# A message-passing layer on one Trainium2 core: scatters and gathers in turn, a shorter start

## The reference, cut to what matters

```
rhat = edge_vec / (norm(edge_vec) + 1e-12);  Y1 = sqrt(3) * rhat
emb  = 8 Gaussians of the clipped length, times sqrt(8), zero where length > 1
w    = mlp(emb)                       # 8 -> 64 -> 64 -> 128, silu between
xs, xv = x[:, :32] @ W_up0, x[:, 32:] as (32, 3) by W_up1   # scaled by 32 ** -0.5
m0 = w0 * xs[src];   m1 = w1 * xs[src] * Y1
m2 = w2 * xv[src];   m3 = w3 * sum_c(xv[src] * Y1) / sqrt(3)
msg = segment_sum([m0, m3 | m1, m2], dst)
out = layernorm(x + (msg_s @ W_out0 | msg_v by W_out1) / (8 * 16))
```

## Time and profile before

| what | us |
|---|---|
| median of 3 runs (1263.23 to 1265.73) | 1265.41 |
| the profiled execution | 1268.42 |
| its span, first to last instruction | 1266.7 |
| POOL busy | 995.5 (79%) |
| PE busy | 968.7 (76%) |
| DVE busy | 698.5 (55%) |
| ACT busy | 540.2 (43%) |

### The profile page before, as it was taken

How to read it: one execution, slowest core, us unless ns; L and a number is a source line. 1 busy time by engine, 2 the same in 40 slices (tenths; PEclk the granted TensorE clock), 3 DMA queues, 4 the chain that set the end, 5 groups by cost and what they waited for, 6 DMA issues and landing times.

```text
span 1266.7 us, 31319 instructions
## 1 busy us (share of the span) xinstructions
PE 968.7 (76%) x6210; PEld 893.6 (71%) x6210; DVE 698.5 (55%) x2916; ACT 540.2 (43%) x1416; POOL 995.5 (79%) x792
## 2 busy tenths in 40 slices
PE   1888888787778887788777777888777868888880
PEld 1787777777777776677677676777676767778770
DVE  6764344466465565556555656646546556555532
ACT  4433223244435434525535534534443543553532
POOL 5378887878888888878888888888888888788885
PEclk9988788888877878878888978779878897777785
DMA  6466674434544444543453454444444454453444
GB/s 204 142 183 181 172 196 78 71 72 97 124 71 98 98 98 71 123 99 70 100 123 73 95 124 70 98 99 82 105 105 74 96 122 72 87 134 43 69 68 89
DMA packets 84975, 132.19 MB, mean 104 GB/s; under 512 B 17308, under 2 KB 69935, under 8 KB 84133
## 3 DMA queue, kind: packets, MB, share of 16 engines
q0 software_dynamic: 68304, 50.25, 29.9%
q1 hardware_dynamic: 14506, 78.09, 17.1%
q10 hardware_dynamic: 1963, 1.71, 0.5%
HBM read 78.35 MB, written 77.24 MB: 123 GB/s over the span
## 4 chain that ended last, share of the span: by engine, by line
POOL 42%; issue 26%; DMA 16%; SPq 10%; POOLq 5%; DVE 0%; ACT 0%
POOL acc L603 28%; DMA acc<-msg,index 14%; POOL sender L573 14%; SPq L380 6%; POOLq L579 3%; SPq L376 2%; SPq L404 2%; DMA acc<-in_x_dram 1%; POOLq L601 1%; POOLq L584 1%; POOLq L602 0%; SPq L426 0%; DMA total<-acc 0%; POOLq L88 0%; SPq L412 0%
## 5 line engine op out<-in xcount | busy, mean ns | idle before, releaser
L603 POOL DMA_INDIRECT acc<-msg,index x391 | 623.5, 1595 | 131.1 <-issue 106.9
L573 POOL DMA_INDIRECT sender<-in_x_dram,index x375 | 368.3, 982 | 128.3 <-issue 102.9
L730 PEld LDWEIGHTS ps_sum<-same,mid 128*128 128x128 f32 x1568 | 255.1, 239 | 10.0 <-DVE mid L1164 0.8
L730 PE MATMUL ps_sum<-same,mid 128*128 128x128 f32 x1568 | 260.2, 321 | 0.7 <-DVE mid L1164 0.7
L1149 DVE TENSOR_TENSOR wts<-ps_wts,bias 128x512 f32<-128x512 f32 x98 | 67.8, 692 | 283.5 <-PE ps_wts L717 283.5
L742 PE MATMUL ps_msg<-outw,sumT 128*128 128x64 f32 x1568 | 220.4, 302 | 0.0
L742 PEld LDWEIGHTS ps_msg<-outw,sumT 128*128 128x128 f32 x1568 | 216.1, 221 | 0.0
L1142 DVE TENSOR_TENSOR proj<-ps_up,vec_all 128x384 f32<-128x384 f32 x98 | 54.4, 555 | 223.5 <-PE ps_up L710 187.9
L827 ACT COPY sumT<-ps_sum 128x512 f32<-128x512 f32 x196 | 115.0, 587 | 146.4 <-PE ps_sum L730 143.7
L689 PE MATMUL ps_sT<-ident,sender 128*128 128x128 f32 x376 | 86.8, 307 | 115.1 <-DMA sender<-in_x_dram,index 114.3
L837 ACT COPY msg<-ps_msg 128x128 f32<-128x128 f32 x98 | 26.1, 266 | 336.1 <-DMA acc<-msg,index 243.1
(11 more groups left out here) (144 smaller groups left out, 1084.6 us busy)
## 6 DMA issues: line engine op xcount, KB each, us to landing
acc<-in_x_dram SPq DMA_DIRECT2D x40, 625.0 KB, 4.8
total<-acc SPq DMA_DIRECT2D x30, 832.0 KB, 4.8
out_dram<-normed SPq DMA_DIRECT2D x29, 832.0 KB
by_row<-in_x_dram SPq DMA_DIRECT2D x1408, 0.5 KB
by_row<-in_x_dram ACTq DMA_DIRECT2D x640, 0.5 KB
acc<-msg,index POOLq DMA_INDIRECT x391, 3.4
sender<-in_x_dram,index POOLq DMA_INDIRECT x375, 6.0
out_dram<-normed ACTq DMA_DIRECT2D x1, 832.0 KB
```

The lines of the kernel that those rows point to most:

```text
L573: pool.indirect_dma_start(sender[:, u % SRING, i, :], None, x, bass.IndirectOffsetOnAxis(ap=index[:, u, 0, i:i + 1], axis=0)).then_inc(fet ...
L603: pool.indirect_dma_start(acc, bass.IndirectOffsetOnAxis(ap=index[:, v, 1, i:i + 1], axis=0), msg[:, v % RING, i, :], None, compute_op=ALU.add
L730: mm = pe.matmul(ps_sum[r][:, i, h, :], mid[:, b, 2 * r + i, P * h:P * (h + 1)], same[:, b, 2 * r + i, :], start=True, stop=True)
```

## The change

1. POOL gathers only the first `EARLY` = 4 units ahead of the first scatter. From then on each scatter of unit v is followed by the gather of the same tile of unit v + 5 (in unit 0, by those of units 4 and 5). The next unit's order is loaded before this unit's scatters.
2. `single_rows` has a twin, `rows_at`, that takes byte offsets. The two lists of row numbers that SP and ACT read in the loop are multiplied by 512 once, on DVE (`scale_ids`). The first two units of SP keep `single_rows`.
3. Basis and directions are made for the first 8 units (`NARROW`) at first, for the other 90 between units 2 and 4. The scatter orders follow unit 0 on DVE (their comparisons are inside it); the output weights are scaled after unit 0's second silu; the message of unit 0 has an order of its own on PE and ACT (`first_message`).
4. SP issues the weights before the zero rows and the first two copies of x, and waits for the turning of unit 1 before the next copies; ACT issues eight of the weight loads. The id lists are loaded after the second pair of copies.

```diff
+EARLY = 4
+NARROW = 8
+ROW_BYTES = D * 4
+        x_bytes = x.rearrange("n d -> (n d)").bitcast(U8)
+        def rows_at(engine, kind, u, i, starts, a, n):
+            _, starts = nc.values_load_multi_w_load_instructions(
+                starts[:, a:a + n], engines=(kind,), min_val=0, max_val=(N - 1) * ROW_BYTES, ...)
+            for p in range(n):
+                engine.dma_start(by_row[a + p:a + p + 1, row_slot(u, i), :].bitcast(U8),
+                                 x_bytes[bass.ds(starts[p], ROW_BYTES)].rearrange("(a d) -> a d", a=1)
                                  ).then_inc(row_in[row_slot(u, i)], 16)
...
 # SP
-            sp.wait_ge(zeroed, 1)
-            sp.dma_start(acc[N:N + SPARE, :]..., zeros[:, :, :]).then_inc(spare_rows, 16)
-            for k in range(PIECES_FIRST):
-                copy(k // 2, k % 2, waits=k >= 2)
             sp.wait_ge(consts, 1)
 # up_raw and mlp0_raw (8 DMAs) now count on loaded_up; then bias2 and out_raw (5) on loaded
-            for s in range(2):
-                (mlp1, mlp2, bias0, bias1)
+            sp.wait_ge(zeroed, 1)
+            sp.dma_start(acc[N:N + SPARE, :]..., zeros[:, :, :]).then_inc(spare_rows, 16)
+            for k in range(PIECES_FIRST):
+                copy(k // 2, k % 2, waits=k >= 2)
             sp.wait_ge(src_in, 16)
+            sp.wait_ge(senderT_ps, 2)
...
-                if h == 2 + P // SP_ROWS:
+                if h == 1:
                     load_ids()
...
 # POOL
-            for u in range(AHEAD):
+            for u in range(EARLY):
...
-            orders = [order_of(v) for v in range(ROW)]
-            for v in range(0, UNITS, ROW):
-                for k in range(min(ROW, UNITS - v)):
-                    begin_scatters(v + k, orders[k])
-                    for i in range(G):
-                        scatter(v + k, i, orders[k] % 2)
-                orders = [order_of(w) for w in range(v + ROW, min(v + 2 * ROW, UNITS))]
-                for u in range(v + AHEAD, min(v + AHEAD + ROW, UNITS)):
+            order = order_of(0)
+            for v in range(UNITS):
+                following = order_of(v + 1) if v + 1 < UNITS else None
+                begin_scatters(v, order)
+                ahead = range(v + AHEAD if v else EARLY, min(v + AHEAD + 1, UNITS))
+                for u in ahead:
                     if u >= SRING:
                         pool.wait_ge(senderT_ps, u - SRING + 1)
-                    for i in range(G):
+                for i in range(G):
+                    scatter(v, i, order % 2)
+                    for u in ahead:
                         gather(u, i)
+                order = following
...
 # PE
-            pe.wait_ge(weights, 6)
-            pe.wait_ge(prepared, 2)
-            pe.wait_ge(loaded, 16 * WEIGHT_DMAS)
+            pe.wait_ge(prepared, 1)
+            def first_message(u, k):
+                hidden0(u, k)
+                sums(u - 1, k - 1, 0)
+                sums(u - 1, k - 1, 1)
+                pe.wait_ge(weights, 6)
+                project_out(u - 1, k - 1)
+                project_up(u, k)
+                hidden1(u, k)
+                radial(u, k)
+                turn(u + 1, k + 1)
...
 # ACT
+            act.wait_ge(consts, 1)
+            for h in range(2):
+                (mlp1, mlp2, bias0, bias1: 8 DMAs, ahead of the planes)
...
+            squares(first, range(NB)).then_inc(act_pre, 1)
+            act.activation(basis_all[:, first, :], basis_all[:, first, :], ACT.Exp, scale=-0.5)
...
+                if k == 0:
+                    scale_out()
...
+                if u == 2:
+                    act.wait_ge(dve_pre, LATER_CLIP)
+                    squares(later, range(NB // 2))
+                if u == 3:
+                    squares(later, range(NB // 2, NB)).then_inc(act_pre, 1)
+                if u == 4:
+                    act.activation(basis_all[:, later, :], ..., ACT.Exp, scale=-0.5)
...
 # DVE
+            def scale_ids():
+                dve.wait_ge(ids_in, 16 * len(ID_LISTS))
+                for ids, units, i, apart in ID_LISTS:
+                    dve.tensor_scalar(ids, ids, float(ROW_BYTES), None, ALU.mult).then_inc(ids_scaled, 1)
...
-            directions()
+            directions(first, 5, 1)
             equal_receivers(0, 0)
-            unit(0, 0)
+            unit(0, 0, following=False)          # compare_tiles() inside it
+            make_scatter_orders()
+            equal_receivers(1, 1)
             unit(1, 1)
+            clip(later, 7)
+            unit(2, 2)
+            unit(3, 3)
+            directions(later, 10, 2)
+            scale_ids()
             make_dense_orders()
-            with dve.Fori(1, PAIRS - 1) as j:
+            with dve.Fori(2, PAIRS - 1) as j:
```

More of the change, by code:

```diff
@@ L794, in _, with squares, scale_out @@
                 mm.then_inc(act_planes, 1)
+            def squares(tiles, of):
+                for k in of:
+                    mm = act.activation(basis_all[:, tiles, k], len_clip[:, tiles], ACT.Square, scale=float(NB - 1),
+                                        bias=minus_k[:, k:k + 1])
+                return mm
+            first, later = slice(0, FIRST_TILES), slice(FIRST_TILES, TILES)
             act.wait_ge(dve_pre, 3)
-            for k in range(NB):
-                mm = act.activation(basis_all[:, :, k], len_clip[:, :], ACT.Square, scale=float(NB - 1),
-                                    bias=minus_k[:, k:k + 1])
-            mm.then_inc(act_pre, 1)
+            squares(first, range(NB)).then_inc(act_pre, 1)
             act.wait_ge(act_pre, 1)
-            act.activation(basis_all[:, :, :], basis_all[:, :, :], ACT.Exp, scale=-0.5).then_inc(act_pre, 1)
-            act.wait_ge(dve_pre, 5)
-            act.activation(norm[:, :], norm[:, :], ACT.Sqrt).then_inc(act_pre, 1)
-            act.wait_ge(loaded, 16 * WEIGHT_DMAS)
-            act.mul(up[:, :], up_raw[:, :], MUL ** -0.5).then_inc(weights, 1)
-            act.mul(mlp0[:, :, :], mlp0_raw[:, :, :], NB ** 0.5).then_inc(weights, 1)
-            by = 1.0 / (AVG * (2 * MUL) ** 0.5)
-            for k in range(4):
-                for h in range(2):
-                    rows = slice(MUL * k, MUL * (k + 1))
-                    y = 3 ** 0.5 if k == 2 or (k == 0 and h == 1) else 1.0
-                    mm = act.mul(outw[rows, h, :], out_raw[rows, h, :], by * y)
-                mm.then_inc(weights, 1)
+            act.activation(basis_all[:, first, :], basis_all[:, first, :], ACT.Exp, scale=-0.5).then_inc(act_pre, 1)
+            def scale_out():
+                act.wait_ge(loaded, 16 * WEIGHT_DMAS)
+                by = 1.0 / (AVG * (2 * MUL) ** 0.5)
+                for k in range(4):
+                    for h in range(2):
+                        rows = slice(MUL * k, MUL * (k + 1))
+                        y = 3 ** 0.5 if k == 2 or (k == 0 and h == 1) else 1.0
+                        mm = act.mul(outw[rows, h, :], out_raw[rows, h, :], by * y)
+                    mm.then_inc(weights, 1)
             def stage(u, k):
@@ L921, in pair @@
                     unit(2 * j + part, k + part, meanwhile=dense, body=body)
+            act.wait_ge(prepared, 1)
+            act.wait_ge(act_pre, 2)
             stage(0, 0)
             stage(1, 1)
+            act.wait_ge(loaded_up, 16 * UP_DMAS)
+            act.mul(mlp0[:, :, :], mlp0_raw[:, :, :], NB ** 0.5).then_inc(weights, 1)
+            act.mul(up[:, :], up_raw[:, :], MUL ** -0.5).then_inc(weights, 1)
+            act.wait_ge(dve_pre, 5)
+            act.activation(norm[:, :], norm[:, :], ACT.Sqrt).then_inc(act_pre, 1)
             turned(0, 0)
```

146 lines of the change are left out of this document (91 added, 55 removed).

## The result

Twenty runs each on one chip: 1268.09 us after (1263.77 to 1271.23), 1265.36 before. The ratio is 1.0018, 95% interval [1.0011, 1.0024], so +2.3 us (+1.4 to +3.0). The forecast was 1261.0, a gain of 4.4; the time lies in its range, but on the other side of no change. The profiled execution took 1265.97, its span 1263.9.

What follows compares the result with a forecast made beforehand. POOL was taken as saturated from its first scatter on. Start -18.5, moved gathers +5.1, wait -2.4, turns +15.8 and long scatters -4.4 gave -4.4 us, from 1265.41 to 1261.0; own range 1252 to 1270, with rivals 1235 to 1286.

Steps and rivals of the forecast that it cites:

- Premise: POOL is saturated, tail 10.6: POOL never pauses noticeably from 54 us to the last scatter; the 10.6 us after that scatter stay unchanged.
- The start, 35.6 and -18.5: First scatter moves from 54.10 to 35.6 us through a shorter ACT, PE and DVE chain: -18.5, bounds 32 to 40.
- late together: Before the first scatter, DVE's scatter orders (34.4) and the message (34.8) were expected ready at nearly the same time.
- Moved gathers +5.1: Unit 4's four gathers move from ahead of the first scatter to behind it, adding 5.1 us to POOL's work.
- wait -2.4: The fourth scatter's 2.68 us wait for the first one's landing goes, as gathers stand between: -2.4 us.
- In turn +15.8: Alternating POOL operations cost 1.60 a scatter and 0.99 a gather, +0.17 us a unit, +15.8 in all.
- long scatters -4.4: Scatters of 1.83 to 1.94 us, all following another scatter, hold 8.8 us; half was counted as gone, -4.4.
- Full price: Every POOL operation in turn pays 1.62 or 1.02 like a first one: +34.4, total 1284.0; chance 0.29.
- One between doesn't unsettle: A single foreign operation on POOL costs nothing: up to -33.5, 1231.9, half way 1240.7; chance 0.25.
- DVE late: DVE's 15 us of work between units 3 and 4 delays message 4: +10 on the forecast, 1271.0; chance 0.12.
- A cache: Scatters and gathers may evict each other from GpSimd's 16 KB instruction cache, making every operation in turn a first one.
- the table switch: At ACT's start the skill's 2.66 us per switch, against 1.28 in the trace, would put the start 1.4 later.

Runs made afterwards that it cites:

- after_again: The kernel after the change, unchanged, run again for a second trace: 1267.51 us, ratio 1.0015 to the kernel before.
- after_third: The kernel after the change, unchanged, run a third time in another set: 1269.56 us, ratio 1.0024 to the kernel before.
- mixed2: runs_early5 with runs of one unit for units 0 and 1, then of two units: 1250.30 us, ratio 0.9872 to the kernel before.
- mixed4: mixed2 with runs of sixteen scatters and sixteen gathers from unit 4, gathers seven units ahead: 1240.57 us, ratio 0.9796 to the kernel before.
- row2: runs_early5 with runs of eight scatters and eight gathers (two units): 1252.07 us, ratio 0.9895 to the kernel before.
- runs_early4: The kernel after with the old runs of four scatters and four gathers, 15 gathers ahead: 1259.51 us, ratio 0.9945 to the kernel before.
- runs_early5: runs_early4 with all 19 gathers ahead of the first scatter, as in the kernel before: 1254.19 us, ratio 0.9900 to the kernel before.
- before_again: The kernel before the change, unchanged, run again for a second trace: 1267.38 us, ratio 1.0004.
- turn_only: The kernel before with only the new POOL order, scatter and gather in turn, 19 gathers ahead: 1274.27 us, ratio 1.0063.
- pairs: The kernel after with two scatters, then two gathers, in place of one each in turn: 1275.02 us, ratio 1.0068 to the kernel before.

## Why the prediction was wrong, by its own steps

- **Premise: POOL is saturated, tail 10.6.** Right: no pause above 0.35 us in after and after_again, one of 1.13 in after_third, tail 10.8 to 10.9.
- **The start, 35.6 and -18.5: this is the step that failed.** It came at 39.3 and was worth 13.5. Two parts:
  - *The base (1.3 of the 5.0).* The 54.10 was a late start; the other two traces of the old start say 51.97 and 52.27. The prediction knew that this execution was 3.0 above the median, but took the whole saving from it and subtracted it from the median of the runs.
  - *The new chain (3.7).* Half of it is the planes. ACT's issues end at 11.2, counted 10.5, but ACT isn't what the planes wait for: the lists didn't land sooner, and ACT's first copy of a plane starts at 13.98. The last ends at 16.71, not 14.5, and these 2.2 are carried on: senderT came at 21.85, not 19.5, DVE's wts at 29.33, not 27.0, mid at 31.65, not 29.3. (The eight small squares took 1.85, not 1.2.) The orders then took 4.8 of the 5.07 and stood at 36.40, not 34.4; in the three traces they are 1.8 late on the mean. The other half, 1.9, lies behind them: POOL began 3.3, 3.1 and 3.1 after the orders, where the forecast had 1.2. The message was not what held it: done at 38.35 in after, because of the lower clock, it cost 0.2 there; in after_again it was done at 36.60, and the scatter still began at 39.35.
- **Behind the orders: a link that the old start hid.** The rows of POOL's queue (ns least, median, most; first and last start) are in the source view, of line 597 in after and of line 579 in before:

```profile
L597 POOLq TENSOR_LOAD <-scatter_orders x98: 283/290/1007, 36.5 to 1233.0; - x98
L597 POOLq FUSED_REGOPS  x98: 152/158/175, 37.0 to 1233.4; - x98
```

```profile
L579 POOLq TENSOR_LOAD <-scatter_orders x98: 288/296/893, 43.6 to 1243.5; - x98
```

  Unit 0's order, and in after unit 1's too, is loaded from DVE's table before the first scatter: two loads and their register operations, begun at 36.5 (36.4 in after_again) and passed by 38.1. What fills the 1.2 us from POOL's last wait to the scatter no view says; in before it was 0.8. Before, the orders were ready at 30.71, over 20 us ahead of the message, and the load at 43.6 ran while POOL waited for that: it cost nothing. The prediction said that the orders and the message would be "late together" and then priced what follows the message, not what follows the orders. It also put the moved load of the next order at nothing; ahead of the first scatter it is a second load in the path, 0.6 us by its rows in after_again (37.2 to 37.75). No run moved `order_of(1)` alone, but mixed2 and mixed4 load only unit 0's order there. mixed2's first scatter began 2.5 after the orders and 0.8 after its last gather, that of row2, which loads two, 4.1 and 1.9. In both the gathers end last, so this is a sign and no measurement.
- **Moved gathers +5.1, wait -2.4.** The first is right: 5.3 between runs_early4 and runs_early5 in time, 3.7 in POOL's term of one trace each. There is no such wait in after and after_again, and one of 0.8 in after_third; before_again had one of 4.0, at 72.41, so the 2.4 too was one trace's.
- **In turn +15.8, long scatters -4.4.** Right in sum: +14.0 for all POOL terms where 14.1 was forecast, and for the order alone 7.2 in POOL's term and 8.0 in time (turn_only) where 15.8 - 4.4 - 2.4 = 9.0 was. That it comes so near is partly luck: two errors cancel. The surcharges don't add by place. The scatter pays 0.018 for one gather between, not 0.05 (1.572, forecast 1.60); the gather pays 0.067 for one scatter between, not 0.04 (1.014, forecast 0.99). As a pair 2.586 against 2.59. The unit in runs was taken a little low, 10.19, from one unit rounded down; by the medians it is 10.22, and +0.125 a unit makes 11.6, not 15.8.
- **Long scatters.** Scatters over 1.75 us were 13 and 9 in the two traces of before, 3 and 9 in after's first two: they didn't vanish with the runs, and gathers over 1.15 us appeared behind the first scatter, 11 and 10 (1 and 1 before). The 8.8 was mis-read too: all that the long scatters hold above 1.57 us is 4.0 and 2.4 in the two traces of before. The 4.4 was a guess that nothing bears out by itself.
- **Rivals.** *Full price*: half true, for the gather (1.014 of 1.02) and not for the scatter (1.572 of 1.62); in time it fell. *One between doesn't unsettle*: half true, the other half. *DVE late*: it didn't happen. The first rival's further +35 is too much as well: the seconds' surcharges, 0.05 a scatter and gather together, make 19 over 93 units.
- **A cache, and the table switch.** The prediction also read the surcharge as the two kinds evicting each other from an instruction cache. That makes every operation in turn a first one, which is the first rival's sum, 1284.0, and not the second's, as the prediction has it. It also makes pairs, with half as many first ones, faster than turns; pairs was 7.5 us slower, so, for whole eviction, that reading falls in this kernel. The Trainium skill ("Advanced Engine Details and Errata", section "Sequencer Memory") gives the cache's size and the length of its lines alone. What makes the surcharge stays open. The Trainium skill ("ScalarE: Activation LUTs", section "What ACT_TABLE_LOAD costs") has about 2.66 us for a switch of sets; the trace does not agree: after's first Sqrt started 1.29 us after its load did (19.98, 21.27).
- **The chances** had 0.11 on no measurable change, where the result nearly lies (+2.3 us, with 2.5 called measurable). Two large terms that nearly cancel, -18.5 and +14.1, should have made that more likely. That the time lies in the stated range shows no more than that the range was wide.

## What to carry to other kernels

When one engine is saturated from its first operation on, its time is a start plus a sum, and the start deserves the same care as the sum: after you pull one input forward, walk the releasing chain of every other input down to the instructions that the engine itself runs between its wait and its work. A start that one trace shows is taken off that trace only, or averaged over several, before it is set against a median. And where a change of kind has a price, try the longest run that the buffers allow, with short runs while the pipeline fills: against runs of four, runs of sixteen took 13 to 14 us off and turns added 8.

## What the chip showed that I had not expected

- The time that POOL takes to prepare an indirect DMA depends on the last two or three operations, and not as a sum. A scatter right behind two gathers takes 1.62, with a scatter between 1.58, right behind a single gather 1.57, and 1.55 among scatters. For a gather a single scatter is nearly the whole price (1.014 of 1.022; among gathers 0.947).
- So the order with the most changes of kind (turns, 1267.5) is faster than the one with half as many (pairs, 1275.0) and slower than one with a quarter (runs_early4, 1259.5).
- The start of one and the same program differs between executions by 2.1 us (before: 51.97 to 54.10), and the landing of the edge lists by 0.6 in the three traces of after (11.27 to 11.87).
